# Experts of a decoder layer: from every token through every expert to sorted tiles of 128 routed rows

## The reference

```python
logits = x @ classifier_weight.T
scores = jax.nn.softmax(logits, axis=-1)
_, topk_idx = jax.lax.top_k(scores + e_score_correction_bias[None, :], K)
topk_w = jnp.take_along_axis(scores, topk_idx, axis=1) * SCALE
w_full = jnp.zeros((T, E_T), jnp.float32).at[jnp.arange(T)[:, None], topk_idx].add(topk_w)
zero_w = w_full[:, E_R:].sum(axis=-1, keepdims=True)
out0 = x * zero_w
def body(out, xs):
    Wgu, Wd, we = xs
    gate, up = jnp.split(x @ Wgu.T, 2, axis=-1)
    y = jax.nn.silu(gate) * up @ Wd.T
    return (out + we[:, None] * y, None)
```

## Time and profile before

| | us |
|---|---|
| median of three runs | 1690.94 (1688.82 to 1693.78) |
| the profiled execution's own time | 1697.1 |
| its span in the trace | 1695.3 |
| TensorE busy in the span | 1550.7 (91%) |
| VectorE busy | 911.0 (54%) |
| ScalarE busy | 906.9 (53%) |
| GpSimd busy | 537.4 (32%) |

### The profile page before, as it was taken

One profiled execution on the slowest core, in us unless ns is written; L12 is line 12 of the kernel. 1 busy time (PEld: TensorE's weight loads), 2 busy tenths in 40 slices (PEclk: granted clock), 3 DMA queues, 4 the chain that ended last, 5 costly groups with the idle time before them and its releaser, 6 DMA issues. The chain is left out here.

```text
span 1695.3 us, 28215 instructions
## 1 busy us (share of the span) xinstructions
PE 1550.7 (91%) x10072; PEld 1016.2 (60%) x10072; DVE 911.0 (54%) x2462; ACT 906.9 (53%) x1622; POOL 537.4 (32%) x588
## 2 busy tenths in 40 slices
PE   6999999999866899899899999459999999999997
PEld 4667667667554433333243322138888888888886
DVE  6665665655528452262145000186777777777775
ACT  5664564654504669768867989423333333333332
POOL 2775665765701355156045100000101010101010
PEclk9999999999978899999999999779999999999999
DMA  6000000000031000010010000200000000000001
GB/s 240 1 14 1 26 14 14 14 2 26 1 90 39 27 27 14 3 58 20 2 40 2 2 26 1 82 10 19 28 19 28 19 28 19 28 19 28 19 19 50
DMA packets 43713, 47.26 MB, mean 28 GB/s; under 512 B 4016, under 2 KB 40384, under 8 KB 43600
## 3 DMA queue, kind: packets, MB, share of 16 engines
q1 hardware_dynamic: 43600, 45.76, 8.6%
HBM read 39.42 MB, written 6.33 MB: 27 GB/s over the span
## 5 line engine op out<-in xcount | busy, mean ns | idle before, releaser
L1162 ACT ACTIVATE xa_probs<-xa_banks 128x1024 f32<-128x1024 f32 (+1 forms) x416 | 400.9, 1045 | 93.3 <-PE xa_banks L1015 92.4
L298 POOL TENSOR_SCALAR sa_probs<-sa_probs,sa_recip 128x128 f32<-128x128 f32 (+3 forms) x256 | 274.9, 1087 | 177.1 <-DVE sa_recip L552 176.8
L1030 PE MATMUL xa_banks<-xa_probs,xa_v_one 128*17 128x512 f32 (+1 forms) x1664 | 223.7, 606 | 8.0 <-ACT xa_q_aug L1110 4.6
L431 ACT ACTIVATE sa_probs<-sa_probs,sa_neg_max 128x128 f32<-128x128 f32 (+3 forms) x256 | 141.9, 555 | 148.2 <-DVE sa_neg_max L489 148.1
L1590 ACT ACTIVATE mo_silu<-mo_banks 128x512 f32<-128x512 f32 x128 | 76.4, 597 | 268.3 <-PE mo_banks L1544 268.3
L1697 DVE SCALAR_TENSOR_TENSOR mo_acc<-mo_banks,mo_current,mo_acc 128x256 f32<-128x256 f32 x512 | 211.6, 476 | 1.4 <-PE mo_banks L1557 1.4
L1544 PE MATMUL mo_banks<-mo_xt_hi,mo_gu_hi 128*128 128x512 f32 x512 | 204.2, 399 | 6.1 <-POOL mo_dn_lo L1488 6.1
L1544 PE MATMUL mo_banks<-mo_xt_lo,mo_gu_hi 128*128 128x512 f32 x512 | 204.2, 399 | 0.0
L1487 POOL TENSOR_TENSOR mo_gu_lo<-mo_gu_raw,mo_gu_hi 128x512 fp32r<-128x512 f32 x32 | 41.4, 1292 | 513.2 <-ACT mo_dn_hi L1599 513.2
L1544 PE MATMUL mo_banks<-mo_xt_hi,mo_gu_lo 128*128 128x512 f32 x512 | 203.0, 397 | 0.0
L1015 PE MATMUL xa_banks<-xa_q_aug,xa_k_aug 32*128 32x512 f32 (+1 forms) x1664 | 155.4, 447 | 21.9 <-issue 9.8
(11 more groups left out here) (205 smaller groups left out, 2685.5 us busy)
## 6 DMA issues: line engine op xcount, KB each, us to landing
mo_gu_raw<-in_gate_up_t SPq DMA_DIRECT2D x32, 256.0 KB, 2.7
xa_raw<-in_ctx_t SPq DMA_DIRECT2D x24, 256.0 KB, 2.8
sa_toeplitz<-extended_bias SPq DMA_DIRECT2D x8, 512.0 KB, 9.3
mo_dn_raw<-in_down_t SPq DMA_DIRECT2D x32, 128.0 KB, 2.5
sa_xn<-in_x SPq DMA_DIRECT2D x4, 512.0 KB, 3.9
sa_x<-in_x SPq DMA_DIRECT2D x4, 512.0 KB, 3.9
x<-sa_x SPq DMA_DIRECT2D x4, 512.0 KB, 2.9
xa_xn<-x SPq DMA_DIRECT2D x4, 512.0 KB, 3.9
```

The source lines that it names most:

```text
L298: pool.tensor_scalar(probs[:, t % SLOTS, 0:w], probs[:, t % SLOTS, 0:w], recip[:, col:col + 1], None, ALU.mult).then_inc(probs_ready, 1)
L431: act.activation(probs[:, t % SLOTS, 0:w], probs[:, t % SLOTS, 0:w], ACT.Exp, bias=neg_max[:, i:i + 1], scale=-1.0, accum_out=sums[:, i:i ...
L1030: last = pe.matmul(banks[32 * i:32 * i + XD + 1, 6 + group % 2, :], v_one[b % 2][0:m, c, 4 * g + i, :], probs[0:m, (2 * j + i // 2) % RING ...
L1162: act.activation(probs[0:m, n % RING, :, :], banks[0:m, 2 * (n % 3):2 * (n % 3) + 2, :], ACT.Exp).then_inc(probs_ready, 1)
```

## The change

`experts` no longer runs every token through every expert. Each pair of a token and a routed expert that it picked becomes a row, and the rows are sorted by expert in DRAM.

- **The router** works by sequence (`pick`, `choose`, `pack`, `normalise` for each of the 4 sequences) in plain fp32. Two matmuls with a triangle of ones and with ones (`rank`) count for each token how many earlier tokens picked the same expert; that gives each of a token's six picks its place in a DRAM tensor `rows`, which has a region of 2048 rows for each expert. A pick of a zero expert goes to a trash place.
- **The scatter**: GpSimd sends each tile's 128 rows (256 values and 18 of bookkeeping, `ROW` = 274) to their places with an indirect DMA, six for each of the 16 tiles, 96 in all.
- **Steering**: from the counts VectorE works out for each of `N_TILES` = 128 tiles at which row it starts and to which expert it belongs (`steer`). 128 tiles always suffice; those that are not needed read blank rows.
- **The tile loop**, written out 128 times, has no loop instruction left. For each tile SyncE reads the row address from SBUF into a register, loads the 128 rows (`xs`), reads the expert's number, and loads that expert's gate-and-up and down weights into one of `W_RING` = 4 slots. TensorE transposes the rows (`turn_rows`, two tiles ahead), makes gate and up (`front`, two fp32 matmuls of 256 columns), transposes the hidden tile (`turn_hidden`) and makes the down product (`back`, one fp32 matmul of 256 columns). VectorE finds each row's weight and destination (`owned`), multiplies (`gate`, `weigh`), and GpSimd scatters each tile of results to a DRAM tensor `parts` with one indirect DMA.
- **The end**: `parts`, six rows for each token, is loaded in 16 DMAs, VectorE sums the six and adds them to `acc`, and four DMAs store it.
- **In `self_attention`** SyncE also clears `rows` (four blocks of 128 rows, 561 KB, at each of the 128 steps) and `parts` (131 KB at each of the first 96), each after a wait on that step's scores. The seven bias pieces and `wo` stand behind the first of them.

The parts of the diff that matter here:

```diff
+REGION = B * T
+N_TILES = TILES * TOP_K + E_ROUTED
+IDLE = 1 + E_ROUTED * REGION
+TRASH = IDLE + P
+SPARE = N_TILES * P
+ROW = D + 3 * TOP_K
...
+                def clear_rows(first, blocks):
+                    sp.dma_start(rows[1 + first * P:1 + (first + blocks) * P, :]
+                                 .rearrange("(n p) w -> p n w", p=P),
+                                 blank[:].unsqueeze(1).to_broadcast([P, blocks, ROW])).then_inc(filled, 16)
                 for s in range(FIRST, LAST):
                     b, i = divmod(s, STEPS)
+                    if 0 <= s < STEPS * B:
+                        if s == 0:
+                            sp.wait_ge(blank_ready, 1)
+                        sp.wait_ge(s_psum, 2 * s + 1)
+                        clear_rows(CLEARED * s, CLEARED)
+                        if s < TILES * TOP_K:
+                            at = SPARE + s * P
+                            sp.dma_start(parts[at:at + P, :], blank[:, 0:D]).then_inc(filled, 16)
                     if s == 0:
+                        clear_rows(CLEARED * STEPS * B, 1)
                         for p in range(1, PAIRS):
                             load_toeplitz(p)
                         sp.dma_start(wo_sb[:], wo.rearrange("(c p) n -> p c n", p=P)).then_inc(wo_in, 16)
...
+    X_RING = 6
+    T_RING = 3
+    H_RING = 3
+    Y_RING = 4
+    AHEAD = 2
+    W_RING = 4
...
-                for i in range(2):
-                    load(i, i)
-                with sp.Fori(0, TURNS - 1) as turn:
-                    for i in range(2):
-                        sp.wait_ge(w_ready, turn * 2 + (i + 1))
-                        load(turn * 2 + (i + 2), i)
-                sp.wait_ge(y_added, 2 + TURNS * PER_TURN)
...
+                sp.wait_ge(steer_ready, 1)
+                sp.wait_ge(sent, 16 * TILES * TOP_K)
+                for t in range(N_TILES):
+                    if t >= X_RING:
+                        sp.wait_ge(t_psum, t - X_RING + 1)
+                        sp.wait_ge(own_ready, t - X_RING + 1)
+                    at = sp.value_load(steer[0:1, t:t + 1], min_val=1, max_val=IDLE)
+                    sp.dma_start(xs[:, t % X_RING, :], rows[bass.ds(at, P), :]).then_inc(xs_in[t % X_RING], 16)
+                    if t >= W_RING:
+                        sp.wait_ge(y_psum, t - W_RING + 1)
+                    e = sp.value_load(steer[0:1, N_TILES + t:N_TILES + t + 1], min_val=0, max_val=E_ROUTED - 1)
+                    own_w = w_ring[t % W_RING]
+                    sp.dma_start(own_w[:, 0:KD * 2 * INTER].rearrange("p (c n) -> p c n", c=KD),
+                                 gate_up_t[bass.ds(e, 1)].rearrange("e (c p) n -> p (e c) n", p=P)
+                                 ).then_inc(w_in[t % W_RING], 16)
+                    sp.dma_start(own_w[:, KD * 2 * INTER:], down_t[bass.ds(e, 1)].rearrange("e p n -> p (e n)")
+                                 ).then_inc(w_in[t % W_RING], 16)
+                for i in range(Y_RING):
+                    sp.wait_ge(y_sent[i], 16 * (N_TILES // Y_RING))
+                for t in range(TILES):
+                    at = SPARE + t * P * TOP_K
+                    sp.dma_start(gathered[:, t * TOP_K * D:(t + 1) * TOP_K * D],
+                                 parts[at:at + P * TOP_K, :].rearrange("(p k) d -> p (k d)", k=TOP_K)
+                                 ).then_inc(parts_in[t], 16)
...
+                for t in range(TILES):
+                    if t % TT == 0:
+                        pool.wait_ge(row_ready, t // TT + 1)
+                    for k in range(TOP_K):
+                        pool.indirect_dma_start(
+                            out=rows, out_offset=bass.IndirectOffsetOnAxis(ap=place_i[:, t, k:k + 1], axis=0),
+                            in_=packed[:, t, :], in_offset=None).then_inc(sent, 16)
+                for t in range(N_TILES):
+                    pool.wait_ge(own_ready, t + 1)
+                    pool.wait_ge(y_ready, t + 1)
+                    pool.indirect_dma_start(
+                        out=parts, out_offset=bass.IndirectOffsetOnAxis(ap=dest[:, t:t + 1], axis=0),
+                        in_=y[t % Y_RING][:], in_offset=None).then_inc(y_sent[t % Y_RING], 16)
...
-                    for half in range(2):
-                        cols = slice(half * INTER, (half + 1) * INTER)
-                        n = 0
-                        for c in range(KD):
-                            for w, u in ((gu_hi, xt_hi), (gu_hi, xt_lo), (gu_lo, xt_hi)):
-                                last = pe.matmul(banks[:, 2 * (j % 2) + half, :], w[i][:, c, cols],
-                                                 u[:, c, tok], start=(n == 0), stop=(n == 3 * KD - 1))
-                                n += 1
...
+                def turn_rows(t):
+                    pe.wait_ge(xs_in[t % X_RING], 16 * (t // X_RING + 1))
+                    if t >= 2:
+                        pe.wait_ge(t_out, t - 1)
                     for c in range(KD):
+                        last = pe.transpose(banks[:, t % 2, c * P:(c + 1) * P],
+                                            xs[:, t % X_RING, c * P:(c + 1) * P], ident[:])
+                    last.then_inc(t_psum, 1)
+                def front(t):
+                    pe.wait_ge(t_out, t + 1)
+                    pe.wait_ge(w_in[t % W_RING], 32 * (t // W_RING + 1))
+                    if t >= 2:
+                        pe.wait_ge(h_ready, t - 1)
+                    for c in range(KD):
+                        last = pe.matmul(banks[:, 2 + t % 2, 0:2 * INTER], xs_t[t % T_RING][:, c, :],
+                                         w_ring[t % W_RING][:, c * 2 * INTER:(c + 1) * 2 * INTER],
+                                         start=(c == 0), stop=(c == KD - 1))
                     last.then_inc(gu_psum, 1)
 
+                def turn_hidden(t):
+                    pe.wait_ge(h_ready, t + 1)
+                    if t >= 2:
+                        pe.wait_ge(ht_ready, t - 1)
+                    pe.transpose(banks[:, 6 + t % 2, 0:P], hidden[t % 2][:], ident[:]).then_inc(ht_psum, 1)
+                def back(t):
+                    pe.wait_ge(ht_ready, t + 1)
+                    if t >= 2:
+                        pe.wait_ge(y_ready, t - 1)
+                    pe.matmul(banks[:, 4 + t % 2, 0:D], hidden_t[t % H_RING][:],
+                              w_ring[t % W_RING][:, KD * 2 * INTER:],
+                              start=True, stop=True).then_inc(y_psum, 1)
+                for t in range(AHEAD):
+                    turn_rows(t)
+                for t in range(N_TILES + 2):
+                    if t < N_TILES:
+                        if t + AHEAD < N_TILES:
+                            turn_rows(t + AHEAD)
+                        front(t)
+                    if 1 <= t <= N_TILES:
+                        turn_hidden(t - 1)
+                    if t >= 2:
+                        back(t - 2)
...
+                def copy_rows(t):
+                    act.wait_ge(t_psum, t + 1)
+                    if t >= T_RING:
+                        act.wait_ge(gu_psum, t - T_RING + 1)
+                    act.activation(xs_t[t % T_RING][:].rearrange("p c n -> p (c n)"), banks[:, t % 2, 0:KD * P],
+                                   ACT.Copy).then_inc(t_out, 1)
...
+                def pack(b):
...
+                    chain.then_wait(dve.tensor_tensor(
+                        same[:], place[:].unsqueeze(2).to_broadcast([P, TT, TOP_K, E_ALL]),
+                        six[:, :, 0:TOP_K].unsqueeze(3).to_broadcast([P, TT, TOP_K, E_ALL]), ALU.is_equal))
+                    chain.then_wait(dve.tensor_tensor(
+                        same[:], same[:], weights[:, tiles(b), :].unsqueeze(2)
+                        .to_broadcast([P, TT, TOP_K, E_ALL]), ALU.mult))
+                    chain.then_wait(dve.tensor_tensor(meta[:, tiles(b), 0, :], six[:, :, 0:TOP_K],
+                                                      trash_at[:, tiles(b), :], ALU.min))
+                    dve.tensor_copy(place_i[:, tiles(b), :], meta[:, tiles(b), 0, :])
+                    dve.tensor_reduce(meta[:, tiles(b), 1, :], same[:], AX.X, ALU.add).then_inc(row_ready, 1)
...
+                def owned(t):
+                    i = t % X_RING
+                    dve.wait_ge(xs_in[i], 16 * (t // X_RING + 1))
+                    chain.then_wait(dve.tensor_scalar(hit[:], xs[:, i, D:D + TOP_K], row_no[:, t:t + 1], None,
+                                                      ALU.is_equal))
+                    chain.then_wait(dve.tensor_tensor(
+                        hits[:], xs[:, i, D + TOP_K:].rearrange("p (a k) -> p a k", k=TOP_K),
+                        hit[:].unsqueeze(1).to_broadcast([P, 2, TOP_K]), ALU.mult))
+                    chain.then_wait(dve.tensor_reduce(own[:, t, :], hits[:], AX.X, ALU.add))
+                    dve.tensor_tensor(dest[:, t:t + 1], own[:, t, 1:2], spare_at[:, t:t + 1], ALU.max
+                                      ).then_inc(own_ready, 1)
```

(26 more changed lines are left out.)

542 lines of the change are left out of this document (292 added, 250 removed).

## The result

The changed kernel takes 2377.3 us (median of 4 runs, 2376.3 to 2379.0) against 1690.6 before: a ratio of 1.406, 95% interval 1.404 to 1.408. The profiled execution's span is 2375.2 us; the prediction's sum for it was 2440.

What follows compares the result with a forecast made beforehand. The prediction took SyncE and TensorE alternating in the tile loop as the bound: 1267.5 us until the scatter landed, 1125 of loop and 47.5 of tail gave 2440 profiled, 2435 as median, range 2210 to 2710.

Steps and rivals of the forecast that it cites:

- The mechanism: Tile loop: SyncE and TensorE alternate, since the next rows' load stands behind a weight-slot wait; TensorE idles 5.5 us a tile.
- router to the first packed rows: Start of the expert stage: load, layernorm, transposes, classifier, choose and pack bring the first packed rows at 1121 us.
- scatter, 96 indirect DMAs and landing: After the first packed rows: GpSimd issues 96 indirect DMAs at 1.5 us, 144 us, plus 2.5 to land, until 1267.5.
- tile loop: 128 tiles at P = 8.9 us each, 5.5 idle plus 3.4 of TensorE's turn at 1.2 GHz: 1125 us in all.
- tail: The end: last scatter 4.5 us, 16 loads paced by VectorE's sum and add at 2.25 each, last store 3: 47.5 us.
- I take 0.7, with 0.1 for the register operations behind it: Tile loop: cost of each of SyncE's two register reads from SBUF, 1.6 us a tile for both; bounds 0.05 and 1.8.
- alternation at full clock: Rival for the tile loop: same alternation with TensorE at 2.4 GHz, P = 7.3 us a tile, total 2235; chance 12%.
- The rival in which VectorE holds up GpSimd's descriptors: Scatter: GpSimd's issues wait through the router, starting at 1181 instead of 1121, 60 us more, 2495; 10%, within the forecast's share.
- The clears cost 0: Self-attention: 84 MB of clears at 190 GB/s fit beside TensorE's work; cost 0, at the upper end 10 us.
- About a fifth of that matmul time: Changed expert stage: its matmul time was put at about a fifth of the old loop's 543 us.
- SyncE's own pace as the next bound: Tile loop, rival without alternation: SyncE's issues and reads set 3.3 us a tile, total about 1750; chance 5%.
- P below 2.9: Tile loop: time per tile (P) under which the kernel gets faster than before; faster rival some 1560 us, chance 3%.

Runs made afterwards that it cites:

- e1: The changed kernel with five weight slots (W_RING = 5) instead of four: 1797.0 us, 1.064 of the time before the change.
- e2: The changed kernel with TensorE transposing rows one tile ahead (AHEAD = 1) instead of two: 1802.7 us, 1.067 of the time before the change.
- e3: The changed kernel with SyncE issuing rows of tile t+2 ahead of its wait for tile t's weight slot: 1717.3 us, 1.016 of before.
- e9: The changed kernel with SyncE's register read ahead of the rows' load done twice in every tile: 2404.1 us, 1.419 of before.
- e10: The changed kernel with 28 useless identity transposes at the head of each TensorE turn, ahead of its wait for rows: 2200.7 us, 1.299 of before.
- e8: e7 with the tail's strided sum over six parts replaced by adds of contiguous elements: 1569.1 us, 0.928 of before.
- e5: The changed kernel with 16 useless identity transposes at the head of each TensorE turn, ahead of its wait for rows: 2233.4 us, 1.321 of before.
- e4: The changed kernel with weights loaded for the first four tiles only, later tiles reusing their slot's content: 2191.4 us, 1.295 of before.
- e11: e8 with the rows issued five tiles ahead instead of four: 1545.7 us, 0.912 of before.
- e6: The changed kernel with six weight slots (W_RING = 6) instead of four: 1695.9 us, 1.004 of before.
- e7: e6 with the rows' register reads and loads moved from SyncE's to ScalarE's queue, four tiles ahead: 1582.2 us, 0.937 of before.

## Why the prediction was right, and where its terms were off

The mechanism was read from the order of the streams and held: turns of equal kind, one gap before the transposes, released by the rows' DMA, none before `front`, SyncE's read for the weights behind the down product. e1, e2 and e3 show it: each changes the order or the distance alone. The sum came out 65 us high, in terms that partly cancel:

| term | predicted | measured | off by |
|---|---|---|---|
| stage starts | 1086.5 | 1078.6 | -7.9 |
| router to the first packed rows | 34.5 | 35.4 | +0.9 |
| scatter, 96 indirect DMAs and landing | 146.5 | 127.7 | -18.8 |
| tile loop | 1125 | 1071.4 | -53.6 |
| tail | 47.5 | 62.1 | +14.6 |

- *Tile loop.* The rest of TensorE was 5.5 in the sum; it is 4.83 between the turn that ends at 1709 and the one that begins at 1713.87. The step that was mis-sized is "I take 0.7, with 0.1 for the register operations behind it": a read is 0.57 with its gaps (e9). From the end of the down product to the issue of gate-and-up it takes 0.75 instead of 0.98, and from the issue of the down weights to that of the rows 1.15 instead of some 1.5. Issue spacing (0.57 for 0.56), landing (2.5) and TensorE's turn (3.46 for 3.4) held. The floor of about 600 ns that the Trainium skill gives for such a read, in DMA: Bandwidth & Descriptors, section "Latency and other measured facts", is close to the 0.57 for the whole read, while the load itself shows 0.27; its figure would have brought the sum 25 us nearer.
- *Clock.* The mean through the loop was 0.60 and not 0.5, and yet TensorE worked at 1.2 GHz, as put: `front` runs at its cold length of 1.9 us in all but 2 of the 128 turns, and its matmuls have a mean of 630 ns, where the fastest takes 379. The time at 2.4 GHz lies in the rests. The clock rose after one turn had ended, with nothing running, and was down again before the next rows landed (stretches; the third is in the next turn's `front`):

```profile
1701.50:1702.50 1.00, 0.00 (x0) 0.00 (x0) 0.00 (x0) 0.00 (x0) 0.87 (x1) 1.00 0.34 45
1704.50:1705.50 1.00, 0.00 (x0) 0.00 (x0) 0.00 (x0) 0.00 (x0) 0.00 (x0) 0.50 0.16 52
1706.50:1707.50 1.00, 1.00 (x4) 0.82 (x3) 0.00 (x0) 0.19 (x1) 0.00 (x0) 0.50 0.00 0
```

  So the mean clock of a stretch doesn't say at which clock the work in it was done. The rival "alternation at full clock" gave 2235; e10, which forces that case, has 2201.
- *Scatter.* An indirect DMA of 128 rows keeps GpSimd for 0.96 us with 0.30 between two, 1.27 and not 1.5. The rival in which VectorE holds up GpSimd's descriptors would have started the scatter at 1181; it started at 1113.9. All 96 (ns min/median/max):

```profile
L1604 POOL DMA_INDIRECT rows<-mo_packed,mo_place_i x96: 956/960/2866, 1113.9 to 1239.1; - x96
```

  A small hold-up shows all the same: VectorE worked until 1176 us, and of the 46 issued by then 11 took 1.00 us or longer, 5 us more than 0.96 each in all; of the 50 after it none did. This agrees with the rule of the Trainium skill on the shared port (SBUF — State Buffer, section "SBUF: two separate sides"), at a twelfth of the 60 us of that rival; no run tests the cause.
- *Tail.* "VectorE's sum over 1536 elements, 1.8 at the rate of 1.21 for 1024" failed: it takes 2.73. An add that reads as many elements contiguously takes 0.95 (e8). Nor is it that a reduction is slow as such: one over contiguous elements in the changed kernel's router takes 1.15 us for 960, which would be 1.8 for 1536. The stride of 256 elements, or the 256 results in place of 24, remains as the reason; no run tells the two apart.

```profile
L1810 DVE TENSOR_REDUCE mo_packed<-mo_same x4: 1145/1146/1147, 1112.5 to 1161.1; 128x24 f32<-128x960 f32 x4
```

- *Self-attention.* The clears cost 0, as put. That the stage behind cross-attention starts 7.9 us earlier than before is no effect of the change: with the same code up to there it starts anywhere from 1074 (e9) to 1086 us (e5) in the traces of this case. The clock between 500 and 1070 us is 0.96 in the late ones, e4, e5, e10 and the kernel before, and 0.97 or 0.98 in the others.
- *Errors that cancel or don't enter.* The router came out within 1 us by luck: the two operations on 960 elements, put at 2.5 us each, take 1.16, and other terms made up for it. "About a fifth of that matmul time" is wrong by the prediction's own numbers: 128 turns of 1.3 us of products and 0.33 of transposes are 209 us of 543, nearly two fifths. e11, at a clock of 0.98, is busy for 229 us. Neither the sum nor the range used the fifth.

The prediction named SyncE's own pace as the next bound if the alternation weren't there, at 3.3 us a tile and about 1750. e6 reaches it at 2.98. Its condition for a faster kernel, P below 2.9, also holds: e6 at 2.98 ends 0.4% above before, e7 at 2.12 far below.

## What to carry to other kernels

Where one queue issues several streams with rings of different depth, the shallowest ring's wait holds up everything written behind it: count, for each transfer, how many turns lie between the event that its predecessors in the queue wait for and its own use. Here a ring of six slots for the rows gave nothing while a ring of four for the weights stood ahead of it; one slot more, or one number less, or another order, was worth 575 to 660 us. And a DMA share near 1 doesn't say that bytes are the bound: leave some out, and issue earlier, and see which of the two moves the time.

## What the runs showed of the hardware that was not expected

- A SyncE register read from SBUF takes 0.27 us, with the register instructions behind it and the gaps 0.57 (e9); in e6, with the DMA engines at a share of 0.75, one took 0.60 for the load alone.
- An issue delayed by 0.57 us cost only 0.2 us a tile, for the rows then landed sooner after it (e9: 2.1 us instead of 2.5).
- Useless transposes in TensorE's gap made the kernel 7% faster (e10), by 1.5 us a turn of clock.
- A reduction over six parts with a stride of 256 elements takes 2.73 us for 1536 elements; an add that reads two times 768 contiguous elements 0.95, a reduction of 960 contiguous ones 1.15.
- TensorE's granted clock can stand at 2.4 GHz in its rests and at 1.2 in its work (the changed kernel's loop: a mean of 0.60, and yet all but 2 of 128 `front` products at their cold length).
